# A two-stage matmul kernel on TensorE: VectorE empties a unit's first bank ahead of the next unit's splits, and the loads and casts of the first units are reordered

## The reference

```python
# layer 0: adapters chosen per batch, rank 16
Bx  = einsum('bni,bri->bnr', x, B[ids0])
x   = x + einsum('bnr,bor->bno', Bx, A[ids0])
# layer 1: W (2048 x 2048) shared, rank-16 pair per batch
base = einsum('bsi,io->bso', x, W)
xr   = einsum('bsi,bir->bsr', x, lora_A[ids1])
x    = x + base + einsum('bsr,bro->bso', xr, lora_B[ids1])
```

## Time and profile before

| | us |
|---|---|
| median of 3 runs | 1305.25 |
| lowest and highest | 1304.99 to 1305.33 |
| the profiled execution, its own time | 1305.84 |
| its span | 1304.1 |
| TensorE busy (matmuls) | 1293.6, 99% of the span |
| VectorE busy | 956.4, 73% |
| ScalarE busy | 458.7, 35% |
| GpSimd busy | 161.0, 12% |

### The profile page before, as it was taken

How to read it: one execution, slowest core, us unless ns; L and a number is a source line. 1 busy time by engine, 2 the same in 40 slices (tenths; PEclk the granted TensorE clock), 3 DMA queues, 4 the chain that set the end, 5 groups by cost and what they waited for, 6 DMA issues and landing times.

```text
span 1304.1 us, 15500 instructions
## 1 busy us (share of the span) xinstructions
PE 1293.6 (99%) x5716; PEld 1068.6 (82%) x5716; DVE 956.4 (73%) x1031; ACT 458.7 (35%) x540; POOL 161.0 (12%) x277
## 2 busy tenths in 40 slices
PE   9999999999999999999999999999999999999998
PEld 7888888888888888888888888887888888888876
DVE  4547766556684686877677866769898887788998
ACT  3322222222234422332232444333433344443451
POOL 3001120111033210001201100111100110100011
PEclk9999999999999999999999999999999999999999
DMA  8886977668999965668978473572965987868467
GB/s 282 270 290 205 314 255 224 229 216 318 377 336 233 295 218 199 212 213 298 362 241 311 172 258 106 192 256 103 256 234 197 369 261 213 228 166 268 122 202 202
DMA packets 87549, 316.33 MB, mean 243 GB/s; under 512 B 15650, under 2 KB 15650, under 8 KB 81074
## 3 DMA queue, kind: packets, MB, share of 16 engines
q1 hardware_dynamic: 61010, 246.44, 54.7%
q0 software_dynamic: 26464, 68.90, 19.1%
HBM read 213.48 MB, written 102.83 MB: 243 GB/s over the span
## 4 chain that ended last, share of the span: by engine, by line
PE 87%; DVE 7%; DMA 2%; issue 2%; ACT 1%; POOLq 0%; POOL 0%; DVEq 0%; ACTq 0%
PE ps L1340 42%; PE ps L2517 34%; PE ps L1289 3%; PE ps L1247 2%; PE ps L2466 2%; DVE xq L2241 1%; PE ps L1268 1%; DVE b_lo L2260 1%; DMA out_y<-stage 1%; PE ps L2452 1%; DMA out_y<-stage_all 1%; DVE stage L2288 0%; DVE w_lo L2254 0%; DMA u<-in_A0n 0%; ACT w_hi L804 0%
## 5 line engine op out<-in xcount | busy, mean ns | idle before, releaser
L1340 PE MATMUL ps<-b_hi,w_hi 128*128 128x512 f32 x888 | 346.0, 390 | 0.4 <-DVE w_lo L968 0.4
L1340 PE MATMUL ps<-b_hi,w_lo 128*128 128x512 f32 x888 | 345.6, 389 | 0.0
L1340 PE MATMUL ps<-b_lo,w_hi 128*128 128x512 f32 x888 | 345.6, 389 | 0.0
L2517 PE MATMUL ps<-b_hi,w_hi 128*128 128x512 f32 x784 | 257.8, 390 | 1.7 <-DVE stage L2288 1.5
L2517 PE MATMUL ps<-b_lo,w_hi 128*128 128x512 f32 x784 | 259.3, 389 | 0.0
L2517 PE MATMUL ps<-b_hi,w_lo 128*128 128x512 f32 x784 | 257.6, 389 | 0.0
L1340 PEld LDWEIGHTS ps<-b_hi,w_hi 128*128 128x128 f32 x888 | 166.7, 188 | 35.8 <-DVE w_lo L968 1.2
L1340 PEld LDWEIGHTS ps<-b_hi,w_lo 128*128 128x128 f32 x888 | 166.7, 188 | 34.7
L1340 PEld LDWEIGHTS ps<-b_lo,w_hi 128*128 128x128 f32 x888 | 166.7, 188 | 34.7
L2087 ACT CAST w_hi<-wq 128x1024 fp32r<-128x1024 f32 x98 | 103.3, 1054 | 208.9 <-PE ps L2517 196.0
L2517 PEld LDWEIGHTS ps<-b_hi,w_hi 128*128 128x128 f32 x784 | 147.0, 188 | 33.7 <-DVE stage L2288 2.7
(11 more groups left out here) (186 smaller groups left out, 1281.9 us busy)
## 6 DMA issues: line engine op xcount, KB each, us to landing
x_raw<-in_xT SPq DMA_DIRECT2D x56, 512.0 KB, 7.3
wq<-w_ops SPq DMA_DIRECT2D x28, 1024.0 KB, 5.1
w_raw<-in_W SPq DMA_DIRECT2D x55, 512.0 KB, 6.8
xq<-in_xT SPq DMA_DIRECT2D x44, 512.0 KB, 6.1
out_y<-stage POOLq DMA_DIRECT2D x38, 512.0 KB, 5.6
w_sum<-x_raw SPq DMA_DIRECT2D x24, 512.0 KB, 8.0
out_y<-stage_all POOLq DMA_DIRECT2D x48, 256.0 KB, 6.1
wq<-w_sum SPq DMA_DIRECT2D x12, 1024.0 KB, 7.3
```

The source lines that it names most:

```text
L1340: last = pe.matmul(bank[:, :], w[n % 2][:, c, t * P:(t + 1) * P], x[:, 2 * j + c, :], start=(j == 0 and c == 0 and w is w_hi and x is b_hi ...
L2517: last = pe.matmul(out, w[:, h, c, col:col + P], b[:, 2 * (q % 2) + c // 2, c % 2, :], start=(po in (Q1, Q2, Q5, Q3) and i == 0), stop=(i ...
```

## The change

VectorE casts W of unit 0 itself, after it has added the identity, and signals that with a new semaphore `first_hi`; ScalarE's list begins with the cast of x, and the counts of `w_hi_done` fall by one everywhere. The waking matmuls are 13 instead of 16. SyncE waits for all eight A0 matrices before it loads W and x of unit 2. In the second stage VectorE's part 1 evictions stand ahead of `w_split` and `x_split`. Nothing is added to or taken from what is computed.

```diff
--- before.py
+++ after.py
@@ -327,6 +327,8 @@
     presum_done = sem("presum_done")
     sum_begun = sem("sum_begun")
     postsum_done = sem("postsum_done")
+
+    first_hi = sem("first_hi")
     w_hi_done = sem("w_hi_done")
     w_ready = sem("w_ready")
     x_hi_done = sem("x_hi_done")
@@ -727,7 +729,7 @@

         for u in range(4):
             if u == 2:
-                sp.wait_ge(w_hi_done, 2)
+                sp.wait_ge(a0_loaded, 16 * NB)
             if u == 3:
                 sp.wait_ge(in_loaded, 32)
             load_raw(u)
@@ -907,7 +909,7 @@
             if n == LAST:
                 break
             due = slot_due(n)
-            if n + 1 < LAST:
+            if 0 < n + 1 < LAST:
                 w_split(n + 1)
             if due:
                 x_split(*due)
@@ -964,7 +966,12 @@
             last.then_inc(presum_done, 1)

         def w_split(n):
-            dve.wait_ge(w_hi_done, n + 1)
+            if n:
+                dve.wait_ge(w_hi_done, n)
+            else:
+                dve.wait_ge(presum_done, 1)
+                dve.tensor_copy(w_hi[0][:, :, :], w_tile(0)[:, :, :]).then_inc(first_hi, 1)
+                dve.wait_ge(first_hi, 1)
             dve.tensor_tensor(w_lo[n % 2][:, :, :], w_tile(n)[:, :, :],
                               w_hi[n % 2][:, :, :].bitcast(F32), ALU.subtract).then_inc(w_ready, 1)

@@ -1300,7 +1307,7 @@

         def first_unit():

-            pe.wait_ge(w_hi_done, 1)
+            pe.wait_ge(first_hi, 1)
             pe.wait_ge(x_hi_done, 1)
             for w, x in ((w_hi, b_hi), (w_lo, b_hi), (w_hi, b_lo)):
                 if w is w_lo:
@@ -1315,7 +1322,7 @@
         def wake():

             pe.wait_ge(eye_done, 2)
-            for _ in range(16):
+            for _ in range(13):
                 pe.matmul(j_ps[:, 0:P], eye[:, :], eye[:, :], start=True, stop=True)

         wake()
@@ -2250,7 +2257,7 @@

         def w_split(n):
             q, h = divmod(n, 2)
-            dve.wait_ge(w_hi_done, F + n + 1)
+            dve.wait_ge(w_hi_done, F + n)
             dve.tensor_tensor(w_lo[:, h, :, :], w_half(q, h), w_hi[:, h, :, :].bitcast(F32),
                               ALU.subtract).then_inc(w_ready, 1)

@@ -2406,13 +2413,13 @@
                 for s in lr_to_read(n, 0, "stage", "u2"):
                     lr_add(s)
                 sums(early_sums(n))
+                for q, t, count, c, begins in evicts(n, 1):
+                    if not by_act(q, begins):
+                        evict(q, t, count, c, begins)
                 if 0 < n and n + 1 < LAST:
                     w_split(n + 1)
                 if n // 2 + 1 < LAST // 2:
                     x_split(n // 2 + 1, n % 2)
-                for q, t, count, c, begins in evicts(n, 1):
-                    if not by_act(q, begins):
-                        evict(q, t, count, c, begins)
                 for s in lr_to_read(n, 1, "stage", "u2"):
                     lr_add(s)
                 if finish(n):
@@ -2503,7 +2510,7 @@
                         terms = [(c, *pair) for c in range(4) for pair in (hi, x_lo, w_lo_)]
                     else:
                         terms = [(c, *pair) for pair in (hi, w_lo_, x_lo) for c in range(4)]
-                        pe.wait_ge(w_hi_done, F + n + 1)
+                        pe.wait_ge(w_hi_done, F + n)
                         pe.wait_ge(x_hi_done, X0 + 2 * q + 2)
                     for i, (c, w, b) in enumerate(terms):
                         if t % 2 == 0 and i == 4:
```

## The result

| us | before | after |
|---|---|---|
| median | 1305.24 | 1318.42 |
| lowest and highest | 1304.99 to 1305.33 | 1316.66 to 1320.40 |
| the profiled execution, its own time | 1305.84 | 1319.76 |
| its span | 1304.1 | 1318.0 |

The ratio of after to before is 1.0095, 95% interval 1.0083 to 1.0107: the change costs 13.2 us. I had predicted 9.4, 1314.7, in a range up to 1318.0. The median lies 0.4 above that range.

What follows compares the result with a forecast made beforehand. TensorE, busy 99% of the span, was taken as the bound. Second-stage losses 4.3+1.7+2.2, M5's end 2.2 and the start's -1.0 summed to +9.4 us: 1314.7 from 1305.25, range 1308.5 to 1318.

Steps and rivals of the forecast that it cites:

- 7.6 for the six products: Second stage before M5: second banks emptied late after third, seventh and eleventh units; 4.3 less 0.60, 1.7 and 2.2 us.
- M5's third unit: Last product, third unit: two splits between two evictions make the second bank late, adding 0.60 us to an existing stall.
- Rival 1: Third units: VectorE's extra work hides in the 1.55 us between evictions, only removed waits count; 1302.3 us, chance 9%.
- less than 2 was to show the prediction wrong: Sign: the prediction is wrong if TensorE's waits in products M1 to M3 stay under 2 us in sum.
- M5's end: Last product: eviction behind a store's landing, both splits behind it, VectorE 2.27 us late; 2.2 us lost, removed stalls swallowed.
- the start: First units: A0 arrives earlier and TensorE's wait for it goes; worth -1.0 us, bounds -1.3 and +0.3.
- the 0.13 of that step: Unit 1 starts at 13.5 instead of 13.63 after earlier first casts: gain 0.13 us, at best 0.3.
- What is late next is unit 2: Start: W and x of unit 2, issued behind A0, ready at 22.6 to 23.9 us; TensorE wants them at 23.67.
- I take no wait: Start of unit 2: TensorE does not wait for its W and x; at the late end 0.3 us.
- the 1.0 itself: Start, unit 1: TensorE's wait for A0 and the slow restart after it disappear, gaining 1.0 us.
- rival 3's first form: Start gains nothing because A0 or unit 2's x lands late, giving back 1.0 us; both forms 1315.7 to 1318, together 18%.
- Its second form: Start: TensorE, idle from 7.1 to 7.8, falls to 1.2 GHz; one or two us more; both forms together 18%.

Runs made afterwards that it cites:

- e3_even: Kernel before with the new eviction order only in third, seventh and eleventh units of the first six products: 1313.76 us, ratio 1.0062, +8.3.
- e4_m5: Kernel before with the new eviction order only in the last product, M5: 1308.06 us, ratio 1.0019, +2.6.
- e1_reorder: Kernel before with only the second stage's part 1 evictions moved, start as before: 1316.63 us, ratio 1.0082, +11.2.
- e2_start: Changed kernel with the second stage's old order, so only the start's part of the change: 1307.17 us, ratio 1.0012, +1.7 against before.
- e8: Kernel before with the new eviction order only in fourth, eighth and twelfth units of the first six products: 1305.88 us against 1306.21, ratio 0.9998.
- e11_less: Kernel before with the difference of the low-rank weights moved ahead of VectorE's part 1 evictions in M5: 1305.64 us against 1305.80, ratio 1.0001.
- e10_start_x: Changed start, old second-stage order, unit 2's loads waiting on ScalarE's second cast of x instead of A0's landing: 1304.71 us against before's 1305.80, ratio 0.9991.
- e9_gate: Kernel before with only SyncE's wait changed: W and x of unit 2 issued once all of A0 has landed: 1310.34 us, one run.
- e12: Kernel before with the changed start, unit 2's loads waiting on ScalarE's second x cast, and M5's low-rank weight difference moved ahead of evictions: 1305.87 us, ratio 0.9997.
- e5_m5_two: Kernel before with the new eviction order only in M5's seventh and eleventh units: 1305.83 us against 1306.21, ratio 0.9994.

## Why the prediction was right, and where it was off

**The mechanism holds, bank by bank.** Lost at the stalls of the first six products, from the steps of TensorE's timeline after (less the 0.227 pace, plus the slow restart, 0.11 and in M7's eighth unit 0.08, less what stood there before):

| unit | worked out | measured |
|---|---|---|
| fourth: M1, M2, M7 | 0.90, 0.88, 0.88 | 0.89, 0.89, 0.89 |
| fourth: M3, M4, M6 | 0.42, 0.23, 0.37 | 0.44, 0.24, 0.37 |
| eighth: M7, M1 | 1.2, 0.5 | 1.27, 0.74 |
| twelfth: M7, M3, M6 | 0.95, 0.95, 0.3 | 0.96, 0.96, 0.30 |

M6's eighth unit lost 0.2 besides. These sum to 8.1. I had 7.6 for the six products (4.3 less M5's 0.60, and 1.7 and 2.2). The runs have 8.3 (e3_even), and the profile 8.6 between 266 us and M5's third unit. Rival 1 needed the splits to hide between two evictions, and they do not: 2.28 us do not go into 1.55. In M1, M2 and M3 the stalls sum to 3.9 us, where less than 2 was to show the prediction wrong.

**M5's third unit** I had at 0.60. Its step went from 0.776 to 1.406, so 0.63.

**M5's end** I had at 2.2, and the reordering alone confirms it: e4_m5 is 2.6 above before, third unit and end together, where my terms say 2.8; e1_reorder's span behind the third unit grew by 2.1 (1315.8 - 1242.53 against 1304.1 - 1232.96). The place was right too: an eviction behind a store's landing, and both splits behind the eviction. What I left out is that the landing has no fixed time. In the changed kernel's profiled execution (GpSimd and ScalarE, VectorE, TensorE):

```profile
1257.52 1.01 POOL L1917 DMA_DIRECT2D out_y<-stage  x1
...
1270.12 0.58 ACT L2112 COPY stage<-ps 128x512 f32<-128x512 f32 x1 [4.27 <-DMA out_y<-stage]
1270.84 0.69 DVE L2295 TENSOR_TENSOR stage<-ps,stage 128x512 f32<-128x512 f32 x1 [4.93 <-ACT stage L2112]
1271.44 1.22 DVE L2261 TENSOR_TENSOR w_lo<-wq,w_hi 128x1024 fp32r<-128x1024 f32 x1
...
1272.72 1.20 PE L2524 MATMUL ps<-b_hi,w_lo 128*128 128x512 f32 x4 [2.58 <-DVE w_lo L2261]
```

The store took 12.5 us instead of 10.1, VectorE idled for 4.93 us, and TensorE ran out of work for 2.58 us in the middle of a tile, for a low half of W that the old order would have had ready. Then its clock fell (stretch and length, busy us of PE, PEld, DVE, ACT and POOL, granted clock, DMA share, GB/s):

```profile
1272.00:1274.00 2.00, 1.28 (x5) 0.82 (x6) 2.00 (x3) 0.00 (x0) 0.00 (x0) 1.00 0.00 0
1274.00:1278.00 4.00, 4.00 (x11) 3.18 (x12) 3.23 (x5) 3.51 (x5) 1.33 (x2) 0.57 0.07 14
1278.00:1282.00 4.00, 4.00 (x19) 3.26 (x19) 3.94 (x6) 2.00 (x2) 0.00 (x0) 1.00 0.94 188
```

For some 3.4 us a matmul took 0.427 us instead of 0.227, eight of them, which is 1.6 us. M5's end is 5.25 us longer than before (76.39 against 71.14 us from the third unit's stall to the end of the span), not 2.2. In the profiled execution this is the term that was mis-sized. Sum of the profiled execution: -0.6 at 266 us, +8.6, +0.6, +5.3: 13.9, which is the difference of the spans. Of the changed kernel's four runs two had a mean granted clock of 1.000 and took 1316.66 and 1317.08; the other two, 0.998 and 0.997, took 1319.76 and 1320.40. That only these two had the fall of the clock is likely; only one of them has a trace that shows it. The medians place the miss otherwise. There M5 costs 2.6 and the six products 8.3, near my 2.8 and 7.6, while the start costs 1.7 where I had -1.0: 12.6 in all, of 13.2 measured. The two views meet in the last product, since what e2_start lost it lost there, behind the same store (below).

**The start** I had at -1.0. It gave 0.5 when unit 2 began, of which 0.3 was left at 265 us; a wait that ends with a store's landing, near 266 us, was another 0.3 shorter. In the medians nothing of it is left. By its steps: the first matmul came at 7.84, as said. The next unit was to start at 13.5 and started at 13.64, no earlier than before. The low half of x was ready at 13.50, and TensorE, done with unit 0 at 13.37, went on 0.14 later. So the 0.13 of that step was not there.

```profile
12.27 1.23 DVE L987 TENSOR_TENSOR b_lo<-x_raw,b_hi 128x1024 fp32r<-128x1024 f32 x1
...
13.64 0.47 PE L1347 MATMUL ps<-b_hi,w_hi 128*128 128x512 f32 x1
```

VectorE's cast, which I took at 1.22, took 0.69:

```profile
6.03 0.69 DVE L973 CAST w_hi<-w_raw 128x1024 fp32r<-128x1024 f32 x1
6.04 0.80 POOL L536 DMA_DIRECT2D u<-in_A0n  x1 [0.58 <-issue]
```

The estimate of 0.7 from the Trainium skill ("VectorE: DVE Perf Modes", the perf-mode tier table) is the measured value. The Trainium skill ("SBUF — State Buffer", "SBUF: two separate sides", the "DVE blocks DMA" trap) spoke against the cast. GpSimd's issue beside it took 0.80 to 1.00 us in the four traces that have the cast and 0.54 in the ten that do not, and the next one came at its usual time. That is the direction of the trap, at 0.3 to 0.5 us and without a consequence. A0 landed at 14.1, the wait at 18.60 is gone: right. "What is late next is unit 2" was right as well, and "I take no wait" was the step that failed. I had followed W and x of unit 2. They were issued 0.9 us earlier than I had said and landed at 18.3 and 19.9, x after 5.4 us, inside my 4.8 to 6.1. Ahead of them on ScalarE stands the cast of the low-rank input:

```profile
19.99 0.71 ACT L852 CAST in_stk<-in_raw 128x256 fp32r<-128x256 f32 x2 [5.14 <-DMA in_raw<-in_A]
...
20.61 1.05 ACT L806 CAST w_hi<-w_raw 128x1024 fp32r<-128x1024 f32 x1
```

This input is issued at 14.46, between W (14.12) and x (14.49) of unit 2. It took 5.5 us and landed at 19.96, where it had been there at 18.36 before. Unit 2 started at 24.19 instead of 23.67. In e2_start it was 24.49. The same instructions start unit 2 between 23.88 and 24.77 in the nine traces of kernels with the old start (before, e1, e3 to e8 and e11), so 0.2 to 0.5 cannot be told from a landing's luck. For the same reason the 1.0 itself was one trace's figure: in those nine TensorE's wait for A0 runs from 0.07 to 0.9 us. This is nearest to rival 3's first form, but the late load was neither A0 nor x of unit 2. Its second form, a fall of the clock near 7 us, did not happen, although the waking matmuls ended at 6.07 and not at 7.1, and TensorE stood idle for 1.77 us and not 0.7. e10_start_x shows what the step should have said: with the low-rank input there by 18.5, unit 2 starts as soon as unit 1 is done.

**What stays open.** e2_start is 1.7 above before although its start is no later. Its profile has the difference in M5's end, where the store took 12.0 us and VectorE idled 2.09 us. Its interval lies above 1, so that one slow execution does not explain it. In the fourteen traces this store took 6.9 to 14.2 us. It took 12.0 to 14.2 in four of the five kernels with a changed start or a changed wait of SyncE (after, e2, e9, e12; e10 has 9.9), and at most 10.6 in the nine others. Whether the start makes it late, 1200 us on, or whether this is chance, the runs do not say. e10_start_x, with nearly the same start, is under before.

## What to carry to other kernels

An eviction moved ahead of other work on an in-order engine does not come early. It comes when its bank is full, and everything that used to fill that wait moves behind it. So compare the work between two evictions with the time until the second bank is wanted, not the first. Where an engine's unbroken work sets the end, removing a wait elsewhere only moves it (e5_m5_two, e11_less). Where a load is moved, follow every landing that stands ahead on the same engine's list, not only the moved ones; and price a wait on a landing by its scatter, not by the one trace at hand.

## What the runs showed of the hardware

- The landing of one 512 KB accumulating store: 9.4 to 14.2 us over twelve traces of nearly the same program, and 6.9 and 7.6 in the two that issue it ahead of two low-rank loads. At 14.2 it made the end of M5 4.0 us longer.
- In the changed kernel TensorE's granted clock was full while the engine stood still for 2.58 us (a step of 2.969), fell 1.5 us after it had started again, to half (from 2.4 to 1.2 GHz), and came back 3.4 us later. Shorter pauses were followed by no fall that the steps show, the longest of them a step of 2.376 us at 1274.03 in e9_gate.
- After a pause of TensorE the second step is 0.305 to 0.341 us instead of 0.227 (0.336 after the 0.62 us in M2, 0.337 after the 2.58 in M5, 0.306 where unit 2 begins). M5's third unit is an exception, with 0.49 to 0.52.
- VectorE casts 128x1024 float32 in 0.69 us, where its subtraction of that size takes 1.22 and ScalarE's cast 1.05.
